# Attention inside a macaron layer: projections in two halves, the fourth group's products in two jobs, other places for outputs, stacks and chains

## What is computed

```python
xn = layernorm(x) * ln_w + ln_b            # of an x that is itself layer-normed
q, k, v = split(xn @ w_qkv, 3)             # 8 heads of 8 features, inner = 64
q, k = q / |q|, k / |k|                    # per head
attn = softmax(causal(8 * q @ k.T))
x = x + concat_heads(attn @ v) @ w_out     # 64 -> 128
```

## Time and profile before

| | |
|---|---|
| median of the runs | 304.62 us |
| profiled execution | 304.3 us, its span 302.5 us |
| TensorE matmul busy | 282.3 us, 93% |
| ScalarE busy | 226.5 us, 75% |
| VectorE busy | 217.9 us, 72% |
| GpSimd busy | 86.0 us, 28% |
| first ffn | from the start to about 121 us |
| attention stage | about 121 to 199 us |
| second ffn | 199 us to the end |

### The profile page before, as it was taken

The page is one execution under the profiler, slowest core; times in us unless marked ns, Lnnn a source line. Parts: engine busy times, 40 slices in busy tenths (PEclk is TensorE's granted clock), DMA queues, the critical chain, the costliest instruction groups (busy, mean ns, idle before and its releaser), DMA issues.

```text
span 302.5 us, 5265 instructions
## 1 busy us (share of the span) xinstructions
PE 282.3 (93%) x1699; PEld 196.8 (65%) x1699; DVE 217.9 (72%) x572; ACT 226.5 (75%) x347; POOL 86.0 (28%) x151
## 2 busy tenths in 40 slices
PE   7699999999999988699998989899999999999994
PEld 7587788688778866133523433258888878878882
DVE  5898979878888876774495361138678797888665
ACT  2476776867787786989797889985677677686672
POOL 6343203302860670451227404121130310310010
PEclk9599999999999999789999999999999999999999
DMA  5710000000000000000000000000000100100101
GB/s 168 218 50 3 0 1 2 0 0 1 2 1 0 3 1 0 2 0 2 0 3 0 3 0 2 0 2 0 2 0 2 35 2 0 35 0 0 36 2 35
DMA packets 8044, 4.66 MB, mean 15 GB/s; under 512 B 626, under 2 KB 8020, under 8 KB 8020
## 3 DMA queue, kind: packets, MB, share of 16 engines
q1 hardware_dynamic: 8020, 4.35, 5.0%
HBM read 3.30 MB, written 1.05 MB: 14 GB/s over the span
## 4 chain that ended last, share of the span: by engine, by line
PE 66%; DVE 9%; POOL 9%; ACT 7%; issue 7%; DVEq 0%; POOLq 0%; ACTq 0%
PE ps L556 9%; PE ps L415 8%; PE ps L425 8%; PE ps L417 7%; PE ps L416 7%; PE ps L427 7%; PE ps L426 7%; PE ps L535 3%; ACT probs L740 3%; DVE h_lo L890 2%; POOL rstd L1125 2%; PE ps L593 1%; PE ps L513 1%; ACT h_hi L730 1%; PE ps L587 1%
## 5 line engine op out<-in xcount | busy, mean ns | idle before, releaser
L727 ACT ACTIVATE h<-ps,cols 128x512 f32<-128x512 f32 x128 | 88.0, 689 | 51.6 <-PE ps L417 45.0
L890 DVE TENSOR_TENSOR h_lo<-h,h_hi 128x512 fp32r<-128x512 f32 x128 | 90.9, 714 | 31.7 <-ACT h_hi L730 28.8
L740 ACT ACTIVATE probs<-ps 128x1024 f32<-128x1024 f32 (+1 forms) x80 | 68.6, 960 | 7.6 <-PE ps L535 7.4
L425 PE MATMUL ps<-h_hi,w_hi 128*128 128x512 f32 x128 | 53.6, 419 | 1.8 <-DVE h_lo L890 1.8
L415 PE MATMUL ps<-xT_hi,w_hi 128*128 128x512 f32 (+1 forms) x128 | 51.8, 405 | 1.4 <-DVE xT_lo L1077 1.4
L417 PE MATMUL ps<-xT_hi,w_lo 128*128 128x512 f32 (+1 forms) x128 | 50.7, 396 | 0.0
L416 PE MATMUL ps<-xT_lo,w_hi 128*128 128x512 f32 (+1 forms) x128 | 50.6, 396 | 0.0
L427 PE MATMUL ps<-h_hi,w_lo 128*128 128x512 f32 x128 | 50.2, 392 | 0.0
L426 PE MATMUL ps<-h_lo,w_hi 128*128 128x512 f32 x128 | 50.0, 390 | 0.0
L730 ACT ACTIVATE h_hi<-ps,cols 128x512 fp32r<-128x512 f32 x72 | 49.1, 682 | 0.0
L1201 POOL TENSOR_SCALAR_AFFINE_SELECT probs<-probs 128x256 f32<-128x256 f32 x64 | 25.9, 427 | 56.4 <-ACT probs L740 55.4
(11 more groups left out here) (127 smaller groups left out, 309.6 us busy)
## 6 DMA issues: line engine op xcount, KB each, us to landing
w_raw<-in_L_ffn_w SPq DMA_DIRECT2D x8, 256.0 KB, 4.7
x_sb<-in_L_attn_x SPq DMA_DIRECT2D x4, 256.0 KB, 7.2
out_x<-x_sb SPq DMA_DIRECT2D x3, 256.0 KB, 2.3
out_x<-x_sb SPq DMA_DIRECT2D x2, 128.0 KB, 1.8
wqkv_sb<-in_L_attn_w_qkv SPq DMA_DIRECT2D x1, 96.0 KB, 4.8
wout_sb<-in_L_attn_w_out SPq DMA_DIRECT2D x1, 32.0 KB, 3.9
small<-in_L_ffn_b SPq DMA_DIRECT2D x1, 8.0 KB
small<-in_L_attn_ln_w SPq DMA_DIRECT2D x1, 0.5 KB
```

Source lines behind the costliest of these rows:

```text
L425: pe.matmul(y, w2_hi[:, w], h_hi[:, c % RING, :], start=(c == 0), stop=False)
L727: first = nc.scalar.activation(h[:, slot, :], ps[:, BANK_H + slot, :], ACT.Gelu, bias=bias)
L740: nc.scalar.activation(probs[:, s % P_SLOTS, :, 0:width], ps[:, bank:bank + 2, 0:width], ACT.Exp, scale=SCALE).then_inc(exp_done, 1)
L890: dve.tensor_tensor(h_lo[:, slot, :], h[:, slot, :], h_hi[:, slot, :].bitcast(f32), ALU.subtract).then_inc(split_done, 1)
```

## The change

The job list is written out anew. `project` of units 1, 3 and 5 becomes two jobs of two tiles each, with a residual add of half the width. `qk` and `v` (four tiles each) are replaced by two jobs `qkv`, of two tiles with all 192 columns each, each emptied by two copies. `rows` 2 moves from quad 16 to 13, straight after its unit. `q_stack` and `k_stack` of the third group move from quads 4 and 5 to 14 and 15, those of the fourth from 17 and 18 to 18 and 19, and `ffn_ln` from 24 to 31. On VectorE the third group's unit vectors and stacks come after `rows` 0, the fourth group's normalisation after `rows` 1, and its chain is cut in three pieces, behind `rows` 2, `q_stack` and `k_stack` of the third group. GpSimd's `ln_twice(LAST)` comes after step 11 in place of step 3.

```diff
--- before.py
+++ after.py
@@ -229,20 +229,18 @@
 
 
 
-        u0, u1, u2, u3 = last_quad[0:4]
-        jobs = [(u0 + 1, "rows", 0), (u0 + 2, "q_stack", LAST - 1), (u0 + 3, "k_stack", LAST - 1),
-                (u1 + 1, "rows", 1), (u1 + 2, "features", 1), (u1 + 3, "project", 1),
-                (u1 + 4, "ln", LAST), (u1 + 5, "qk", LAST), (u1 + 6, "v", LAST), (u2 + 4, "rows", 2),
-                (u2 + 5, "q_stack", LAST), (u2 + 6, "k_stack", LAST)]
-        for u in range(3, len(units) - 1):
-            at = last_quad[u] + 1
-            jobs.append((at, "rows", u))
-            if u % 2:
-                jobs += [(at + 1, "features", u), (at + 2, "project", u)]
-        jobs.append((last_quad[4] + 2, "ffn_ln", 0))
-        jobs.sort(key=lambda j: j[0])
+        u0, u1, u2, u3, u4, u5, u6, u7 = last_quad
+        jobs = [(u0 + 1, "rows", 0),
+                (u1 + 1, "rows", 1), (u1 + 2, "features", 1), (u1 + 3, "project", (1, 0)), (u1 + 4, "project", (1, 1)),
+                (u1 + 5, "ln", LAST), (u1 + 6, "qkv", 0), (u1 + 7, "qkv", 1),
+                (u2 + 1, "rows", 2), (u2 + 2, "q_stack", LAST - 1), (u2 + 3, "k_stack", LAST - 1),
+                (u2 + 6, "q_stack", LAST), (u2 + 7, "k_stack", LAST),
+                (u3 + 1, "rows", 3), (u3 + 2, "features", 3), (u3 + 3, "project", (3, 0)),
+                (u4 + 1, "rows", 4), (u4 + 2, "project", (3, 1)),
+                (u5 + 1, "rows", 5), (u5 + 2, "features", 5), (u5 + 3, "project", (5, 0)), (u5 + 4, "project", (5, 1)),
+                (u5 + 6, "ffn_ln", 0), (u6 + 1, "rows", 6)]
         u = len(units) - 1
-        jobs += [(quad_steps, "rows", u), (quad_steps, "features", u), (quad_steps, "project", u)]
+        jobs += [(quad_steps, "rows", u), (quad_steps, "features", u), (quad_steps, "project", (u, None))]
         assert len({at for at, *_ in jobs}) == len(jobs) - 2
         job_number = {(kind, arg): n for n, (_, kind, arg) in enumerate(jobs)}
 
@@ -312,7 +310,7 @@
             if p < LAST:
                 eng.wait_ge(qkv_copied, p + 1)
             else:
-                eng.wait_ge(job_emptied, job_number["qk", p] + 1)
+                eng.wait_ge(job_emptied, job_number["qkv", 1] + 1)
             if p:
                 eng.wait_ge(stack_done, 2 * p)
             eng.wait_ge(newton_done, NEWTON_OPS * (p + 1))
@@ -574,13 +572,10 @@
                     pe.wait_ge(xn_done[norm], GROUP_TILES * (LAST + 1 if kind == "ln" else GROUPS + 1))
                     for i, tile in enumerate(tiles):
                         m = pe.transpose(bank[:, tile], xn[:, norm, i, :], ident[:, :])
-                elif kind == "qk":
-                    for tile in tiles:
-                        m = pe.matmul(bank[:, tile], xf[:, ATT, tile], wqkv_sb[:, 0:2 * INNER], start=True, stop=True)
-                elif kind == "v":
-                    for i, tile in enumerate(tiles):
-                        m = pe.matmul(bank[:, INNER * i:INNER * i + INNER], xf[:, ATT, tile],
-                                      wqkv_sb[:, 2 * INNER:3 * INNER], start=True, stop=True)
+                elif kind == "qkv":
+                    for i in halves[arg]:
+                        m = pe.matmul(bank[:, 192 * (i % 2):192 * (i % 2) + 192], xf[:, ATT, tiles[i]], wqkv_sb[:, :],
+                                      start=True, stop=True)
                 elif kind == "rows":
                     pe.wait_ge(o_copied, arg + 1)
                     for tile in tiles:
@@ -589,7 +584,7 @@
                     for i, tile in enumerate(tiles):
                         m = pe.transpose(bank[0:INNER, tile], o_tok[:, i, :], ident[:, :])
                 elif kind == "project":
-                    for tile in tiles:
+                    for tile in tiles if arg[1] is None else [tiles[i] for i in halves[arg[1]]]:
                         m = pe.matmul(bank[:, tile], o_feat[:, tile], wout_sb[:, :], start=True, stop=True)
                 m.then_inc(job_filled, 1)
 
@@ -921,7 +916,7 @@
                                   ALU.mult, ALU.add).then_inc(seed_done, 1)
 
             def own_squares(p):
-                dve.wait_ge(job_emptied, job_number["qk", p] + 1)
+                dve.wait_ge(job_emptied, job_number["qkv", 1] + 1)
                 dve.tensor_tensor(sq[:, :, :], qk_raw[:, :, :], qk_raw[:, :, :], ALU.mult).then_inc(sq_done, 2)
 
             def stacks(p):
@@ -1038,12 +1033,13 @@
                     dve.wait_ge(qkv_mm, LAST)
                     dve.tensor_scalar(xf[:, ATT, :], bank, cols[:, COL_LNW:COL_LNW + 1], cols[:, COL_LNB:COL_LNB + 1],
                                       ALU.mult, ALU.add).then_inc(job_emptied, 1)
-                elif kind == "qk":
-                    dve.wait_ge(qkn_done, 2 * arg)
-                    dve.tensor_copy(qk_raw[:, :, :].rearrange("p t c -> p (t c)"), bank).then_inc(job_emptied, 1)
-                elif kind == "v":
-                    dve.tensor_copy(v_ones[:, 4 * arg:4 * arg + 4, :, 0:HEAD_DIM],
-                                    bank[:, 0:GROUP_TILES * INNER].rearrange("p (t h d) -> p t h d", t=GROUP_TILES, h=HEADS)
+                elif kind == "qkv":
+                    dve.wait_ge(qkn_done, 2 * LAST)
+                    qkv = bank[:, 0:384].rearrange("p (t c) -> p t c", t=2)
+                    t0 = GROUP_TILES * LAST + halves[arg][0]
+                    dve.tensor_copy(qk_raw[:, halves[arg][0]:halves[arg][1] + 1, :], qkv[:, :, 0:2 * INNER])
+                    dve.tensor_copy(v_ones[:, t0:t0 + 2, :, 0:HEAD_DIM],
+                                    qkv[:, :, 2 * INNER:3 * INNER].rearrange("p t (h d) -> p t h d", h=HEADS)
                                     ).then_inc(job_emptied, 1)
                 elif kind == "ffn_ln":
                     dve.wait_ge(gate_mm, GROUPS)
@@ -1062,9 +1058,11 @@
                 elif kind == "features":
                     dve.tensor_copy(o_feat[:, :], bank[0:INNER, :]).then_inc(job_emptied, 1)
                 elif kind == "project":
-                    t0 = SEQ // P * units[arg][0] + GROUP_TILES * units[arg][1]
-                    xi = x_sb[:, t0:t0 + GROUP_TILES, :].rearrange("p t d -> p (t d)")
-                    dve.tensor_tensor(xi, bank, xi, ALU.add).then_inc(job_emptied, 1)
+                    u, half = arg
+                    t0 = SEQ // P * units[u][0] + GROUP_TILES * units[u][1]
+                    first, end = (0, GROUP_TILES) if half is None else (halves[half][0], halves[half][1] + 1)
+                    xi = x_sb[:, t0 + first:t0 + end, :].rearrange("p t d -> p (t d)")
+                    dve.tensor_tensor(xi, bank[:, P * first:P * end], xi, ALU.add).then_inc(job_emptied, 1)
 
             dve.memset(v_ones[:, 0:TILES // 2, :, HEAD_DIM + 1:ROW].rearrange("p t h r -> p (t h) r"), 0.0).then_inc(v_zero, 1)
             dve.wait_ge(x_in[0], 16)
@@ -1088,8 +1086,6 @@
             wait_stats(ATT, LAST)
             aggregate(ATT)
             inverse_lengths(dve, LAST - 1)
-            unit_vectors(dve, LAST - 1)
-            stacks(LAST - 1)
             for n, (_, kind, arg) in enumerate(jobs[:-3]):
                 if kind == "ffn_ln":
                     normalise(FFN, GROUPS, 0)
@@ -1097,15 +1093,20 @@
                     copy_o(arg)
                 empty(n)
                 if (kind, arg) == ("rows", 0):
+                    unit_vectors(dve, LAST - 1)
+                    stacks(LAST - 1)
+                if (kind, arg) == ("rows", 1):
                     normalise(ATT, LAST, LAST)
-                if kind == "v":
+                if (kind, arg) == ("rows", 2):
                     own_squares(LAST)
                     square_sums(LAST)
+                if (kind, arg) == ("q_stack", LAST - 1):
                     guesses(LAST)
+                if (kind, arg) == ("k_stack", LAST - 1):
                     inverse_lengths(dve, LAST)
                     unit_vectors(dve, LAST)
                     stacks(LAST)
-                if (kind, arg) == ("project", 1):
+                if (kind, arg) == ("project", (1, 1)):
                     dve.wait_ge(job_emptied, n + 1)
                     first_stats(GROUPS)
                 if kind == "ffn_ln":
@@ -1200,7 +1201,7 @@
                     region = probs[:, s % P_SLOTS, :, at:at + P]
                     pool.affine_select(region, region, [[0, 2], [1, P]], ALU.is_ge, 0.0, base=0,
                                        channel_multiplier=-1).then_inc(mask_done, 1)
-                if s == 3:
+                if s == 2 * last_quad[1] + 1:
                     ln_twice(LAST)
                 if s == 2 * last_quad[3] + 1:
                     ln_once(GROUPS)
```

## The result

The changed kernel is slower: 305.27 us median against 304.36 for the kernel before, ratio 1.0035, 95% interval 1.0026 to 1.0044. The forecast was 302.9, a gain of 0.6%. The measured time lies inside the range, but on the other side of no change, and it is nearest to rival (a), 304.9.

The account below looks back on a forecast made before the run. The attention stage was taken as a race of ScalarE's exponentials and TensorE's lumpy jobs. -2.1 up to quad 16, +2.2 up to quad 24, -1.8 behind make -1.7: 302.6 by profile, 302.9 by median; range 302.1 to 305.5.

Parts of the forecast that it names:

- rival (a): Clock falls near 162 in the new q_stack stall, half until 169, 2.0 us lost: 304.9 us; chance 0.36.
- a wait of about 3 us at q_stack: TensorE stands 3.2 us from 160.4 for the fourth group's stacks, ending 163.6; ScalarE idle 2.7 us.
- no wait at rows 2: Rows 2, moved to quad 13, finds its output copy done at 151.8; the 1.33 us TensorE stall goes.
- no idle of ScalarE from quad 33 on: Quad 33's first exponential starts at 184.4 instead of 186.09; from there ScalarE runs without idle, as before.
- The clock holds: The forecast case, granted clock not falling in the new stall: 302.9 us, own range 302.2 to 303.7; chance 0.44.
- Up to the stall: Chain starts at 157.3, takes 6.30 us, ends at 163.6; ScalarE idle until 164.55.
- half of a job's time for half a job: Project 1.09 becomes twice 0.55; qkv jobs cost 0.64 each, saving TensorE 0.87 us, bounds 0.5 to 0.9.
- the gain of 1.8 us that I booked there: Behind quad 24, project halves and ffn_ln at quad 31 cut ScalarE's idle from 2.9 to 1.1 us.
- Rival (b): Chain before q_stack better hidden, stall 2 us or less, 1 us more gain: 301.8 us; chance 0.07.
- Rival (c): Halves cost more than half, gain behind the stall shrinks to nothing, stall stays: 304.6 to 305.0 us; chance 0.13.
- the third group's stacks cost nothing before the first output: Start of the stage: VectorE's third-group stacks move behind unit 0's output copy; that edit is hidden, worth 0.

Follow-up runs that it names:

- e3: Changed kernel plus twelve unused 512-column matmuls on TensorE before its wait for the fourth group's stacks: 304.28 us, ratio 1.0005 to the kernel before.
- e4: Changed kernel with one of three Newton rounds for the fourth group's inverse lengths (less exact, a test only): 301.75 us, ratio 0.9918 to the kernel before.
- e10: The kernel of e9 plus thirteen unused matmuls in TensorE's idle stretches between 121.9 and 127 us: 300.62 us, ratio 0.9895 to the kernel before.
- e9: The kernel of e5 with the fourth group's stack jobs at quads 18 and 19, second-layer statistics behind that chain: 300.85 us, ratio 0.9893 to the kernel before.
- e1: Changed kernel with only its halves and late ffn_ln kept; stacks, VectorE chains and rows 2 in the old order: 306.38 us, ratio 1.0074 to the kernel before.
- e11: The kernel of e9 with the three project pairs as one whole job each: 301.13 us, ratio 0.9917 to the kernel before.
- e7: Changed kernel with the three project pairs put back to one job of four tiles each: 305.45 us, ratio 1.0058 to the kernel before.
- e6: The kernel of e5 plus thirteen unused matmuls in TensorE's idle stretches between 121.9 and 127 us: 303.43 us, ratio 0.9993 to the kernel before.
- e8: Changed kernel with the former qk and v jobs in place of the two qkv jobs: 305.36 us, ratio 1.0051 to the kernel before.
- e5: Changed kernel, fourth group's norm and products ahead of unit 1's features and project, third group's stacks at quads 4, 5: 304.23 us, ratio 1.0013 to before.
- e2: Changed kernel with third group's stacks back at quads 4 and 5, fourth group's chain in one piece behind rows 2: 304.42 us, ratio 1.0017 to before.

## Why the prediction was wrong

The method found the mechanism and its place: a wait of about 3 us at q_stack ended by VectorE's stacks (3.2 forecast, 3.46 measured), no wait at rows 2, no idle of ScalarE from quad 33 on. The likeliest case failed all the same, by 187.71 - 184.4 = 3.3 us at quad 33, in three terms. (By the medians it is 2.6: -1.7 was forecast and +0.9 measured, in part since half of the changed kernel's runs had a better clock than the profiled one.)

The clock, 1.2 us. "The clock holds" had 0.44, its fall 0.36. It fell, and e3 shows what that costs: 1.2 us in the profile and at equal clock, 0.9 by the ratios. My price for the rival was 2.0, with the fall near 162, before the work; it came at 166.6, when TensorE had worked at full clock for 1.5 us after the stall, and lasted 3.4 us and not the 6.8 that I had taken. The argument that dense products before and after would hold the clock up was wrong. The Trainium skill ("TensorE: Matmul & The Clock Gate", the section on oscillation) says that a wait between two bursts of matmuls makes the gate fall back, so that the next burst starts at the low clock. The trace of the change agrees on the fall, with 1.86 us for 1.00 at 168.20, but not on its moment: there the burst started at 1.00.

Up to the stall, 1.4 us, of which the halves are the greater part that can be named. I took half of a job's time for half a job. A project half costs 0.64 (143.06 to 143.70), not 0.55, and a qkv half 0.85 (148.79 to 149.64), not 0.64, which is above my own upper bound for the pair of 1.57. Two of each make 0.6. TensorE was at k_stack at 156.96 in place of 156.1, so the chain began at 158.22 for 157.3, 0.9 late, of which 0.3 is not placed, and it took 6.7 in place of 6.3 us. That makes 1.3, and 1.4 at quad 22: 165.94 for 164.55.

Behind the stall, 0.7 us. From quad 22 to 33 I had 19.85, e3 and e4 measure 20.58, and the kernel before 20.8. Some 0.2 of this is ahead of quad 24: quad 22 to quad 24 took 3.95 us in e3, in my walk 3.75, before 2.9, since after a stall ScalarE starts with no lead and a job beside a quad shows as an idle of 0.4 to 0.5. The other 0.5 is behind it. From quad 24 to quad 33 the changed kernel and e3 both took 16.6 us, before 17.9: of the gain of 1.8 us that I booked there 1.3 was there. By start-to-start times its gaps were 0.1 to 0.4 larger than in the walk, in part by the same size of a half.

Rival (b) is out, since the wait was 3.46. Rival (c) would have been the better forecast with the clock up: e3 is at 1.0005. It was right that a half costs more than half, but not that the gain behind the stall shrinks to nothing. Rival (a) is what happened, with a part of (c); the two are not exclusive, and I had priced each as if the other's term were right. That the measured 305.27 is near (a)'s 304.9 is partly luck: (a) has 0.8 too much for the clock and lacks the 2.1 of the other two terms. The parts of the chance of a gain add up to 0.52, not 0.51. The statement that the third group's stacks cost nothing before the first output fits the clock of that stretch, and e10 shows a wait of 0.7 us at the old order once the clock is up.

## What to carry to other kernels

When an order is changed, write down for each chain when its first input is there and how long it is, and place the reader by that: e9 has the changed kernel's jobs and differs from it mainly by where the chain starts (147 for 154) and where it is awaited; the third group's stacks and the second layer's statistics stand elsewhere too, and together that is worth 4.4 us. Smoothing the jobs of an engine brings little while a stall stands behind them, as the engine only reaches the stall sooner (e1 lost 2.4 us, with a later chain and a fall of the clock); without the stall the same halves bring something (e11). A stall on TensorE is not over with its end: look at the granted clock behind it. And price a split job by a measured small one, not by division.

## What was not expected of the hardware

The clock fell 1.5 us after TensorE had resumed work from a 3.46 us idle, and not in it. In other profiles it fell 0.2 us after the end of the stall (e1 and e7) or 1.0 to 1.1 us (e6 and e8), each time for 3.4 us. The length of the stall alone does not decide it: the clock fell behind 1.73 us in e6's profile, and held behind the same 1.73 us in e5's and behind 2.5 us in e2's.

The mean clock differs between runs of the same program: 0.970 or 0.975 in the changed kernel, with 0.8 us between the medians, and 0.977 or 0.982 to 0.987 in the kernel before, with 0.9. That need not be the fall behind the stall. The first dip has two lengths in the profiles, 6.8 us in the kernel before, the changed kernel and e9, and 3.4 us in e3, e7 and e8; and e7 and e8, which keep the stall of 3.46 us, have the fall behind it at mean clocks of 0.983 and 0.975. Which dip was short in which of the other runs their mean clock does not tell.

Four records of 128x192 float32 products took 0.85 us by themselves, and eight of them 1.27 in one job: if the rest grows with the records, that is a fixed part of some 0.4 us for a job, an estimate from these two. For the project's 64x128 records it is 0.64 against 1.09, so about 0.2.

The twelve operations of Newton's method took 3.10 us before and 3.66 in the changed kernel (158.22 to 161.88), single ones 0.3 in place of 0.2. The slow ones, from 158.22 to 159.6 and from 160.92 to 161.6, are those beside GpSimd's masks (157.15 to 159.5 and 160.77 to 161.6), and those beside its root computation between them took 0.2; whether the masks are the cause was not tried.
